# A decoder layer on one core: last tile's FFN rows in buffers of their own, T2 computed already turned, T1's weights in two transfers, and a new order of the instructions

## The reference, cut to what matters

```python
x = layernorm(x + attn(x))        # 16 heads of 16; logits against 64 latent keys; top 4, softmax; plus V; Wo
x = layernorm(x + xattn(x, ctx))  # 16 heads; scores of q_r against k_r over 64 context rows; softmax; Wo
x = layernorm(x + ffn(x))         # h = silu(lin(x, w1, g1)) * lin(x, w2, g2);  lin(h, w3, g3)

# xattn
q_big = einsum('bshk,hkq->bshq', (x @ Wq.T).reshape(b, s, H, K), w_kc_q)
scores = einsum('bhsr,bhlr->bhsl', einsum('bshq,hqr->bhsr', q_big, W_qr),
                                   einsum('bld,hdr->bhlr', kv_rope, W_kr))
# lin: rmsnorm with gain g, rows rounded to 8 bits by their largest value, times ternary weights
```

## Time and profile before

| | |
|---|---|
| time, median of 3 runs | 338.94 us (338.52 to 338.99) |
| time of the profiled execution | 339.06 us |
| its span | 337.3 us |
| instructions | 7205 |
| PE busy | 315.6 us, 94% of the span, 2392 instructions |
| PEld busy | 228.5 us, 68% |
| ACT busy | 283.0 us, 84% |
| DVE busy | 280.3 us, 83% |
| POOL busy | 247.9 us, 73% |
| transfers | 22.29 MB, most of it before 45 us |

### The profile page before, as it was taken

The page is one execution under the profiler, slowest core; times in us unless marked ns, Lnnn a source line. Parts: engine busy times, 40 slices in busy tenths (PEclk is TensorE's granted clock), DMA queues, the critical chain, the costliest instruction groups (busy, mean ns, idle before and its releaser), DMA issues. The chain is left out here.

```text
span 337.3 us, 7205 instructions
## 1 busy us (share of the span) xinstructions
PE 315.6 (94%) x2392; PEld 228.5 (68%) x2392; DVE 280.3 (83%) x717; ACT 283.0 (84%) x535; POOL 247.9 (73%) x234
## 2 busy tenths in 40 slices
PE   8999988999899998999999999999998999989972
PEld 4786766687777865777778757776685777466441
DVE  1497568957879999999997899999997878988882
ACT  2686899994759889989897999999896899998873
POOL 3367536884878997898889797969794965668661
PEclk9999999999999999999999999999999999999999
DMA  6999800000000001120101140020220213111001
GB/s 222 400 421 415 315 15 2 0 4 2 0 2 1 17 16 31 33 47 4 33 16 33 32 34 17 17 63 0 49 47 33 33 33 78 31 32 35 14 20 47
DMA packets 24853, 22.29 MB, mean 66 GB/s; under 512 B 19824, under 2 KB 22256, under 8 KB 23920
## 3 DMA queue, kind: packets, MB, share of 16 engines
q1 hardware_dynamic: 24816, 21.84, 21.2%
HBM read 15.01 MB, written 2.10 MB: 51 GB/s over the span
## 5 line engine op out<-in xcount | busy, mean ns | idle before, releaser
L589 PE MATMUL small<-V_sb,PT_sb 128*128 128x256 f32 x256 | 58.3, 381 | 0.8 <-ACT PT_sb L872 0.8
L589 PEld LDWEIGHTS small<-V_sb,PT_sb 128*128 128x128 f32 x256 | 48.0, 190 | 9.4 <-issue 2.5
L554 PE MATMUL wide<-B_sb,x1T 128*128 128x512 f32 x192 | 49.6, 407 | 2.9 <-ACT PT_sb L872 1.5
L1379 POOL TENSOR_TENSOR Ls<-Ls,m 128x1024 f32<-128x1024 f32 x16 | 31.2, 1948 | 26.9 <-DVE mask L1122 26.9
L1108 DVE MAX8 m<-Ls 128x8 f32<-128x64 f32 x256 | 33.9, 210 | 13.8 <-ACT Ls L802 13.5
L554 PEld LDWEIGHTS wide<-B_sb,x1T 128*128 128x128 f32 x192 | 35.4, 188 | 13.2 <-ACT PT_sb L872 3.1
L1444 POOL TENSOR_TENSOR region_c<-region_c,region_q 128x1024 f32<-128x1024 f32 (+1 forms) x17 | 33.3, 1959 | 9.1 <-DVE region_c L1233 6.8
L1394 POOL TENSOR_TENSOR Ls<-Ls,mask 128x1024 f32<-128x1024 f32 x16 | 37.9, 2366 | 2.5 <-ACT Ls L815 1.8
L1386 POOL TENSOR_TENSOR mask<-mask,r 128x1024 f32<-128x1024 f32 x16 | 32.3, 2019 | 2.6 <-DVE r L1131 2.5
L613 PE MATMUL wide<-tern,region_k 128*128 128x512 bf16 x128 | 32.6, 379 | 0.6 <-ACT region_k L926 0.3
L1417 POOL TENSOR_TENSOR P<-P,r 128x1024 f32<-128x1024 f32 x16 | 30.5, 1904 | 1.1 <-DVE r L1177 1.1
(11 more groups left out here) (190 smaller groups left out, 836.7 us busy)
## 6 DMA issues: line engine op xcount, KB each, us to landing
region_q<-in_wqx SPq DMA_DIRECT2D x1, 2048.0 KB, 17.6
region_c<-in_woTx SPq DMA_DIRECT2D x1, 2048.0 KB, 10.7
out_x<-region_q SPq DMA_DIRECT2D x16, 128.0 KB, 1.9
first<-in_xT SPq DMA_DIRECT2D x7, 256.0 KB, 8.6
region_c<-in_wkcqT SPq DMA_DIRECT2D x1, 1536.0 KB, 11.8
region_r<-in_wqkr SPq DMA_DIRECT2D x1, 1024.0 KB, 7.5
region_r<-in_w1T SPq DMA_DIRECT2D x1, 1024.0 KB, 12.8
region_t<-in_w2T SPq DMA_DIRECT2D x1, 1024.0 KB, 14.8
```

The lines of the kernel that those rows point to most:

```text
L554: mm = pe.matmul(ps_L2[:, r * 512:(r + 1) * 512], x1T[:, u, k, :], B_sb[:, s, w, k, r * 512:(r + 1) * 512], start=(u == w == k == 0), stop ...
L589: mm = pe.matmul(ps_O2[:, 0:D], PT2_sb[:, c, :], V_sb[:, c, :], start=(c == 0), stop=(c == PAIRS - 1))
L1379: pool.tensor_tensor(heads(Ls[n % 2][:]), heads(Ls[n % 2][:]), over_heads(m8[:, :, 0:1]), ALU.subtract).then_inc(g_d1, 1)
```

## The change

1. T2. `T2_` now takes a head's 128 columns of `wkcqT` as the stationary operand and streams T1's 64 columns. The result is 128 x 64 per head, the layout that `A_` reads. `keep_T2`, `T2T` and their semaphores are gone; one ACT copy (`copy_T2`) is left. The loop goes head pair by head pair, and within it over u and then e.
2. T1. The transfer of `wqkr` is cut in two, one for each half of the pairs c, each with a semaphore. `T1_(0)` waits for the second half only when it comes to it. `T1_(1)` writes another bank (wide 2 and not wide 1).
3. The last tile. `xg`, `xqT`, `th`, `hh`, `hg` and `hqT` of tile 15 get memory of their own in places that are dead by then (parts of `first`, the mask, one of the two `Ls`), and its waits for tile 14 are dropped; some waits for the last readers of that memory come in.
4. Banks. `ps_WF`, `ps_WB`, `ps_S3` are exchanged between the small banks; tile 15's `XQT` and first half of `HT` use small bank 0.
5. Order. The lists of all five engines are new. The same steps are in them, but for those dropped. The `warm` instructions are 18 in the head (15 before) and 30 at the end (35 before).

```diff
-            sp.dma_start(region_r[:], a["wqkr"]).then_inc(ld_T1, 16)
+            for i in range(2):
+                sp.dma_start(halves_r[:, i], a["wqkr"][:, i]).then_inc(ld_T1[i], 16)
...
-                for i in range(PAIRS // 2):
+                for c in range(PAIRS):
                     for u in range(2):
-                        for e, c in ((0, i), (1, i + PAIRS // 2), (1, i), (0, i + PAIRS // 2)):
+                        for e in range(2):
                             h, rows = e * PAIRS + c, slice(e * DC, (e + 1) * DC)
-                            mm = pe.matmul(ps_T2[rows, c * HK:(c + 1) * HK],
+                            mm = pe.matmul(ps_T2[:, h * DC:(h + 1) * DC],
+                                           wkcqT[1][rows, c, :] if u else wkcqT[0][:, h, :],
                                            T1[1][rows, c * DC:(c + 1) * DC] if u else T1[0][:, h * DC:(h + 1) * DC],
-                                           wkcqT[1][rows, c, :] if u else wkcqT[0][:, h, :],
                                            start=(u == 0), stop=(u == 1))
                 mm.then_inc(p_T2, 1)
-
-            def T2T(*freed):
-
-                bank_of(*freed)
-                pe.wait_ge(c_ident, 2)
-                pe.wait_ge(a_T2k, 1)
-                for c in range(PAIRS):
-                    mm = pe.transpose(ps_T2T[:, c * P:(c + 1) * P], T2_kept[:, c * HK:(c + 1) * HK], ident[:])
-                mm.then_inc(p_T2T, 1)
...
+        def home(n, own, last):
+
+            return last if n == TILES - 1 else own
...
-                pool.tensor_tensor(hg[:, cols], hh[:, cols], g3[:, cols], ALU.mult).then_inc(g_hg, 1)
+                if n < TILES - 1:
+                    since(pool, d_hT, 16 * min(n, TURNED))
+                    since(pool, p_HT, n - TURNED)
+                pool.tensor_tensor(home(n, hg, hg_last)[:, cols], home(n, hh, h_and_eps_last)[:, cols],
+                                   g3[:, cols], ALU.mult).then_inc(g_hg, 1)
```

More of the change, by code:

```diff
@@ L199, in decoder_layer @@
         ps_XQT = small[1]
+        ps_XQT_last = small[0]
         ps_HT = small[0]
@@ L955, in whole_h @@
                 act.wait_ge(v_sqh, n + 1)
-                act.activation(hg[:, columns(half)], hg[:, columns(half)], ACT.Copy, bias=ROUND,
+                row = home(n, hg, hg_last)[:, columns(half)]
+                act.activation(row, row, ACT.Copy, bias=ROUND,
                                scale=ch[:, 2:3]).then_inc(a_qh, 1)
@@ L1023, in _ @@
[L1023 to L1027 removed]
+            spread_lat_v(); copy_Q(0); copy_L1(0); copy_T1(0); copy_T1(1); exp_4(0); copy_L1(1)
@@ new lines, in _ @@
+            exp_4(7); pack_x(0); copy_B(2, 1); copy_B(3, 1); copy_V(1, 1); square_2(1)
+            norm_1(5); exp_1(7); copy_AT(6); copy_PT2(2); norm_2(1); tanh(0); copy_V(0, 1)
+            exp_4(8); square_x2(1); exp_2(4); square_2(2); copy_PT2(3); whole_x2(1); square_1(6)
+            pack_x(1); norm_2(2); square_x2(2); copy_X1(5); square_h(0); copy_V(1, 2)
+            copy_PT1(7); copy_L1(9); exp_1(8); whole_h(0); copy_AT(7); pack_h(0); whole_x2(2)
+            tanh(1); pack_x(2); exp_2(5); norm_1(6); copy_PT1(8); square_2(3); square_3(0)
@@ new lines, in _ @@
+            copy_L1(10); copy_X1(6); square_1(7); copy_AT(8); square_h(1); norm_2(3)
+            copy_PT2(4); tanh(2); exp_4(9); norm_1(7); copy_V(0, 2); square_x2(3); square_1(8)
+            exp_1(9); whole_h(1); pack_h(1); copy_Q(6); square_h(2); whole_x2(3); pack_x(3)
+            exp_2(6); copy_PT2(5); square_3(1); norm_1(8); copy_X1(7); copy_PT1(9); whole_h(2)
+            tanh(3); square_2(4); pack_h(2); norm_2(4); copy_B(0, 2); copy_X1(8); exp_1(10)
+            exp_4(10); square_x2(4); copy_L1(11); square_2(5); exp_2(7); copy_AT(9); whole_x2(4)
@@ new lines, in _ @@
+            pack_x(4); norm_2(5); copy_PT2(6); copy_V(1, 3); square_x2(5); copy_V(0, 3)
+            copy_PT1(10); copy_B(1, 2); copy_B(2, 2); square_3(2); copy_B(3, 2); square_h(3)
+            exp_4(11); copy_AT(10); exp_1(11); square_1(9); norm_1(9); copy_L1(12); copy_Q(7)
+            whole_h(3); pack_h(3); tanh(4); square_1(10); exp_2(8); exp_4(12); copy_PT2(7)
+            whole_x2(5); pack_x(5); square_2(6); square_h(4); copy_PT1(11); copy_X1(9)
+            norm_1(10); square_3(3); copy_L1(13); norm_2(6); exp_1(12); whole_h(4); pack_h(4)
@@ new lines, in _ @@
+            copy_X1(10); square_2(7); square_x2(6); copy_V(1, 4); copy_AT(11); exp_2(9)
+            copy_V(0, 4); copy_PT1(12); tanh(5); whole_x2(6); square_1(11); copy_PT2(8)
+            pack_x(6); norm_1(11); exp_1(13); copy_AT(12); norm_2(7); square_x2(7); exp_4(13)
+            square_3(4); copy_L1(14); square_h(5); square_1(12); tanh(6); whole_h(5); pack_h(5)
+            copy_PT2(9); square_2(8); copy_X1(11); norm_2(8); whole_x2(7); exp_4(14)
+            copy_PT1(13); pack_x(7); square_x2(8); square_h(6); exp_2(10); exp_1(14); whole_h(6)
@@ new lines, in _ @@
+            copy_B(0, 3); copy_AT(13); tanh(7); square_2(9); norm_1(12); pack_h(6); copy_L1(15)
+            square_3(5); copy_PT1(14); copy_V(1, 5); whole_x2(8); copy_X1(12); square_1(13)
+            copy_B(1, 3); copy_AT(14); pack_x(8); copy_B(2, 3); copy_B(3, 3); square_h(7)
+            norm_1(13); exp_2(11); copy_V(0, 5); copy_PT2(10); tanh(8); square_1(14); norm_2(9)
+            exp_1(15); square_x2(9); exp_4(15); square_3(6); copy_PT2(11); whole_h(7); pack_h(7)
+            square_2(10); whole_x2(9); pack_x(9); copy_X1(13); square_h(8); norm_2(10)
@@ new lines, in _ @@
+            exp_2(12); square_x2(10); copy_PT1(15); copy_V(0, 6); tanh(9); copy_AT(15)
+            norm_1(14); whole_h(8); pack_h(8); square_3(7); whole_x2(10); square_2(11)
+            copy_X1(14); exp_2(13); pack_x(10); norm_2(11); copy_PT2(12); square_h(9)
+            square_x2(11); copy_V(1, 6); square_1(15); square_3(8); whole_h(9); pack_h(9)
+            tanh(10); norm_1(15); exp_2(14); whole_x2(11); pack_x(11); copy_PT2(13)
+            square_2(12); square_h(10); norm_2(12); square_x2(12); copy_X1(15); whole_h(10)
@@ L1503, in _ @@
[L1503 to L1508 removed]
+            shift_1(2); scale_mask(2); weights_1(2); root_1(0); shift_1(3); scale_mask(3)
@@ L1511, in rope_tables @@
+            root_2(15); gain_x(15); roots_x(15); gain_h(13); roots_h(13); root_3(11); gain_h(14)
+            roots_h(14); gain_h(15, 0); root_3(12); gain_h(15, 1); roots_h(15); root_3(13)
+            root_3(14); root_3(15)
 def rope_tables():
```

467 lines of the change are left out of this document (214 added, 253 removed).

## The result

The changed kernel takes 341.80 us (median of 4 runs, 341.31 to 342.42) against 338.88 beside it; the ratio is 1.0089, interval 1.0066 to 1.0112. It is 2.9 us slower, and the forecast was 2.8. The size is right by luck, by two misses that cancel: the head lost far more than summed, and the middle gave far more back. The profiled execution took 342.27 us with a span of 340.5.

A forecast was written before the change was run, and what follows sets the result against it. PE was taken to bound the kernel, busy 94% of the span. Terms +2.15 + 1.2 + 1.2 - 1.4 - 0.4 = +2.75 us on 339.06 gave 341.8 us, own range 340 to 344, full range 336.3 to 344.3.

The forecast's parts named there:

- T2, +2.15: T2 in the head: 3.5 + 1.8 + 2.5 us, taken as 7.7, against 5.55 before with T2T; 2.15 us slower.
- The first rival: T2's changes of form are hidden, T2 takes 5.3 us, total 339.4 us, no measurable change; chance 0.16.
- The head, +1.2: Around T2: T2 waits for wkcqT until 14.7 us, Q(1) follows it; PE 1.2 us behind, bounds 0.9 to 1.6.
- Up to 60 us, +1.2: Behind the head: PE waits 3.8 us for ACT's copies, against 2.6 before; 1.2 us slower, bounds -1.1 to +2.4.
- The middle, -1.4: 60 to 300 us: half of 2.8 us in three PE holes closed by the order; bounds -5 to +2.
- the second rival: New order closes most of the middle's 8.1 us of holes, winning over 4.2; 337.7 us at -5.5; chance 0.28.
- The third named hole: In the middle: PE's 0.62 us wait at PT1(13), 199.99 us, goes as it moves away from the bank it awaited.
- The sign set for this: PE's busy time from 60 to 300 us, shifted by the lag: below 231 the sum holds, above 235 the second rival.
- The end, -0.4: Last tiles: 1.4 us gained by tile 15's own memory, 1.0 lost by ACT's order; net -0.4, bounds -2 to +0.8.
- The half on whole_h(12) ahead of norm_2(15), +1.0: At the end, on ACT: whole_h(12) delays norm_2(15), then POOL's gains and all that follow, by 1.0 us.
- The third rival: At the end norm_2(15) is not on the path: -1.4 and not -0.4, 340.8 us; within the forecast's 0.56.
- The gain forecast as -1.4: At the end: own memory brings whole_h(15, 0) about 1.6 us before its 328.55; counted as -1.4 us.

The follow-up runs named there:

- the two grouped kernels: Changed kernel with T2's products grouped by form: one change of form, 335.76 us (ratio 0.9895), and seven changes, 336.71 us (0.9924).
- G = 8: Changed kernel with T2's loop turned inside out, all u = 0 products before u = 1, one change of form: 335.76 us, ratio 0.9895.
- the other two: Q(1) put ahead of T2 on the changed kernel, 340.86 us (ratio 1.0044), and on the changed kernel with the old T2, 334.01 us (0.9850).
- g8_again: Changed kernel with T2 grouped to one change of form, the same kernel as G = 8 run again as base: 336.08 us.
- after_old_t2: Changed kernel with the old T2, T2T and the two copies put back into its new order: 334.86 us, ratio 0.9871.
- before_new_t2: Kernel before, in its own order, with the new T2 (15 changes of form) and without T2T: 344.11 us, ratio 1.0152.
- after_q1_first: Changed kernel, T2 with its 15 changes of form, with Q(1) put ahead of T2: 340.86 us, ratio 1.0044.
- g8_shared_rows: g8_again with tile 15's rows back in the shared buffers and its waits for tile 14 back: 343.14 us, ratio 1.011.

## Why the prediction was right, and where its steps were not

**T2, +2.15.** The sum 3.5 + 1.8 + 15 changes is confirmed at full clock: 7.65 us by the two grouped kernels, against 7.7. In G = 8 the 32 loads of 128 rows take 3.6 us and the 32 of 64 rows 1.9. A change costs 0.143 where 0.17 was taken. The bounds from -0.25 to +4.8 were left all the same: T2 cost 10.89 - 5.55 = +5.3, as the granted clock fell to 0.50 in the middle of it, 3.2 us, and Q(1) behind it paid 1.15 more. This is the step that failed: the sum priced each instruction at its duration at full clock and never asked whether the new series of instructions would keep that clock. The first rival (the changes hidden) is refuted. The Trainium skill, TensorEngine Tiling (Array Packing), "When to Use Tiling", advises the swap and column tiling that the kernel before has, and names a tiling factor of 2 for 64 columns. Here T2 alone took 6.51 us without the swap and 4.69 with it, both with 7 changes, 1.4 times as long; and T2T, which the swapped result needs, cost 0.87 more.

**The head, +1.2.** Confirmed in cause (wkcqT lands at 14.32) and near in price: T2 started at 14.36, 1.05 us earlier than before where 0.7 was forecast, and Q(1)'s 1.92 behind it leaves +0.9 in this trace. Q(1) ahead of T2 gave back 1.2 us on the grouped form and 0.9 on the other two (1.1 and 0.65, if each is held against the kernel before beside it). Of B_(0,0)'s 8.2 us, 5.3 + 1.15 + 0.9 are T2, Q(1) at the low clock and this term; 0.67 is PE's wait for DVE ahead of B_(0,0), which the prediction didn't have, and the last 0.15 lies in WF, PT1(0), WB and Q(2), a little longer or shorter each. That the split transfer wins nothing by itself stands in the traces; the times leave up to 1.2 us open.

**Up to 60 us, +1.2.** It didn't come. C_(0) waited 1.11 us for the copy of L1, where 1.5 at least was forecast, but L2(0), which had waited 1.34 for B, waited for nothing, and WT(2) ahead of it 0.58: together 1.7 against 2.6. Counted in finished steps, each at its duration before, PE is as far at 68.6 us as it had been at 60.8: 7.8 behind, where it was 8.2 at B_(0,0). It is the same in g8_again, 1.8 and 2.2, so it isn't the long lag that hid the wait. The step let all of ACT's work in the stretch stand between B_(3,0) and C_(0); which part of it was done earlier wasn't traced.

**The middle, -1.4.** It was -3.9, close to the second rival's condition (over 4.2) and inside the bound of -5. The mechanism was the forecast one, holes that the order closes: PE's wait of 1.31 us at O3(7) and of 0.83 at O2(14) are gone, and so in after_old_t2, which wins the same 4.3 us from B_(0,0) to O2(15). The third named hole, PT1(13)'s 0.62, is gone as well, but new ones opened at the same kind of step (1.25 us ahead of a PT1 at 101.67). In g8_again PE is busy 234.33 us from 62.2 to 302.2, against 231.91: 2.4 us of the holes. The sign set for this, below 231 or above 235, thus came out between. From B_(0,0) to O2(15) the two traces hold the same steps of PE, so the win can be split: PE is idle 7.6 us in g8_again and 11.0 before, 3.4 less, and busy 261.6 and 262.4, 0.8 less. The term was mis-sized by counting only the named holes and halving them.

**The end, -0.4.** Measured -0.7 in the span (from O2(15) to the end 33.5 us, before 34.2). The half on whole_h(12) ahead of norm_2(15), +1.0, is refuted with its sign: going back costs 0.7 us. The prediction looked at what norm_2(15) delays and not at what is queued behind norm_2(15) while it waits itself. The third rival is right in that nothing is lost there. The gain forecast as -1.4 shows in part: whole_h(15, 0) starts 24.7 us behind O2(15) (331.69), and had started 25.5 behind it (328.55), 0.8 earlier and not 1.6. What of that the buffers of their own did can't be read apart in this order.

In sum: +5.3 + 1.15 + 0.9 + 0.8 - 0.4 - 3.9 - 0.7 = +3.15, the span's +3.2. Forecast was +2.75. Slower was right. That the size was near is luck: 4.3 us more were lost at T2 and Q(1), where the sum had no term for the clock, against 3.9 us more won in the rest.

## What to carry to other kernels

Where PE bounds the whole kernel, a reordering is worth what holes it closes, and a microsecond lost in the head is paid in full at the end; so change the head and the order in separate steps, or the one hides the other (here -4.4 us behind +6.9). When a loop alternates between forms of products and nothing forbids another order, group each form: in T2 it took one loop turned inside out, and left alone it cost 2.0 us of changes and 4.4 us of clock. Before a latency is filled with products of zeros, look whether real work stands behind the step that waits.

## What of the hardware was not expected

The granted clock of PE can fall to 0.50 in a stretch in which the rows show PE busy all the time (3.00 of 3.00 us, 5.20 of 5.20), in T2's series of products of 64 columns with a change of form after every fourth instruction. It fell in T2 in the traces of all three kernels with this loop unfilled (the changed one, before_new_t2, after_q1_first), and all 14 executions of these have a mean clock of 0.980 to 0.989. In no trace did it fall in a T2 with 7 changes or 1, nor with two products of zeros of 512 columns after each 16 instructions. But T2's loop isn't the only place: in after_old_t2 and g8_shared_rows the clock fell in T1, also a series of products of 64 columns, behind a wait of 0.56 us, while in the other traces T1 kept it. And two of the 46 executions of the kernel before took 342.43 and 342.57 us with a mean clock of 0.987, without a trace that would show where. The Trainium skill, TensorE: Matmul & The Clock Gate, "Why this matters for your kernels", names stretches in which PE stands idle as what to avoid in the middle of a kernel; by that rule alone the clock would have stayed in T2, and the rows here show that a busy PE isn't enough.

A weight load of 128 float32 columns takes 0.19 us in the rows, yet in G = 8 T2's 64 loads and products were done in 5.65 us, 0.11 us for each load of 128 rows and 0.06 for each of 64: loads overlap, and their duration isn't their price.
